# Two attention and expert layers on one core: the expert stage in two parts, its tiles in the order of steps of the attention

## The reference: what is computed

```python
# attention of layer 0; layer 1 has biases and the mask for rope
q = (x @ Wq).reshape(B, Nq, H, hd).transpose(0, 2, 1, 3)
kv = (context @ Wkv).reshape(B, Nkv, 2, H, hd).transpose(2, 0, 3, 1, 4)
q, k, v = _apply_rope(q), _apply_rope(kv[0]), kv[1]
attn = jax.nn.softmax(jnp.einsum('bhqd,bhkd->bhqk', q, k) * scale, axis=-1)
out = jnp.einsum('bhqk,bhkd->bhqd', attn, v).transpose(0, 2, 1, 3).reshape(B, Nq, C) @ Wo + bo

# experts of layer 0
probs = jax.nn.softmax(tokens @ Wr + br, axis=-1)
expert = jnp.argmax(probs, axis=-1)
h = jax.nn.relu(jnp.einsum('td,edh->teh', tokens, W1) + b1[None])
y = jnp.einsum('teh,ehd->ted', h, W2) + b2[None]   # the row of `expert`, times its probability

# experts of layer 1
topk_vals, topk_idx = jax.lax.top_k(gate_logits, 2)
probs = jax.nn.softmax(topk_vals, axis=-1)
g = jax.nn.silu(jnp.einsum('btc,hc->bth', x, w_gate_proj[e]))
u = jnp.einsum('btc,hc->bth', x, w_up_proj[e])
out = out + jnp.einsum('bth,ch->btc', g * u, w_down_proj[e]) * w_e[..., None]

# the whole
x = x + tanh(g_xattn[0]) * L0_xattn(layernorm(x), ctx)        # rotary q and k, softmax over 77 keys
x = x + tanh(g_ffn[0])   * L0_ffn(layernorm(x))               # best expert: relu(t @ W1 + b1) @ W2 + b2, times its probability
x = x + tanh(g_xattn[1]) * L1_xattn(layernorm(x), ctx, mask)  # biases, a mask
x = x + tanh(g_ffn[1])   * L1_ffn(layernorm(x))               # two best experts: (silu(g) * u) @ Wd, weighted
```

## Time and profile before

| | us |
|---|---|
| median of three runs | 472.65 (469.25 to 473.23) |
| the profiled execution | 466.07 |
| its span in the trace | 464.2 |
| PE busy | 314.7 (68%) |
| DVE busy | 264.1 (57%) |
| POOL busy | 152.2 (33%) |
| ACT busy | 136.3 (29%) |
| data moved | 52.93 MB, mean 114 GB/s |

### The profile page before, as it was taken

How to read it: one execution, slowest core, us unless ns; L and a number is a source line. 1 busy time by engine, 2 the same in 40 slices (tenths; PEclk the granted TensorE clock), 3 DMA queues, 4 the chain that set the end, 5 groups by cost and what they waited for, 6 DMA issues and landing times.

```text
span 464.2 us, 7008 instructions
## 1 busy us (share of the span) xinstructions
PE 314.7 (68%) x1932; PEld 228.1 (49%) x1932; DVE 264.1 (57%) x916; ACT 136.3 (29%) x302; POOL 152.2 (33%) x172
## 2 busy tenths in 40 slices
PE   2468999989754095751467999999530298888920
PEld 2236555545353094640256566654320297777820
DVE  2768668773675244353367667765545066665634
ACT  2412354535313033220103454354200033333300
POOL 3211212051423134561102102165766134555550
PEclk9767799999985579795567999999855599999985
DMA  7434032100000867823231313000103677988708
GB/s 268 126 74 118 12 80 52 43 11 19 17 8 29 224 215 215 243 73 90 62 85 36 71 27 85 14 24 23 42 29 100 213 244 236 299 249 289 235 12 269
DMA packets 39997, 52.93 MB, mean 114 GB/s; under 512 B 7177, under 2 KB 24334, under 8 KB 39968
## 3 DMA queue, kind: packets, MB, share of 16 engines
q1 hardware_dynamic: 33648, 45.03, 33.7%
q0 software_dynamic: 3584, 6.36, 3.9%
q10 hardware_dynamic: 2736, 1.20, 0.9%
HBM read 35.58 MB, written 9.64 MB: 97 GB/s over the span
## 4 chain that ended last, share of the span: by engine, by line
PE 21%; DVE 8%; issue 7%; DMA 6%; SPq 4%; POOL 4%; ACT 1%; POOLq 0%; DVEq 0%; ACTq 0%
POOL routed L445 3%; PE ps_s L750 2%; PE ps_a L730 2%; DMA xt<-routed 2%; PE ps_a L731 2%; PE ps_s L821 2%; SPq L342 2%; PE ps_s L751 2%; PE ps_t L705 2%; PE ps_n L765 2%; PE ps_a L838 1%; PE ps_d L765 1%; PE ps_t L821 1%; DMA probs<-expert_out 1%; DMA routed<-pay,slot 1%
## 5 line engine op out<-in xcount | busy, mean ns | idle before, releaser
L463 POOL DMA_INDIRECT expert_out<-yo,rows_at x64 | 63.0, 984 | 81.5 <-DVE yo L1179 63.6
L529 ACT ACTIVATE probs<-ps_s 103x512 f32<-103x512 f32 (+1 forms) x96 | 56.3, 597 | 56.8 <-PE ps_s L751 53.3
L445 POOL DMA_INDIRECT routed<-pay,slot x48 | 48.4, 1009 | 58.3 <-DVE slot L1132 47.8
L1025 DVE TENSOR_REDUCE negm<-ps_a 128x4 f32<-128x308 f32 x128 | 55.1, 470 | 19.5 <-PE ps_a L731 18.0
L750 PE MATMUL ps_s<-qs,ks 128*103 128x512 f32 (+1 forms) x96 | 46.2, 481 | 2.0 <-ACT augT L522 1.2
L731 PE MATMUL ps_a<-ks,qs 128*128 128x308 f32 x128 | 43.1, 374 | 5.9 <-DVE negm L1025 5.6
L421 POOL TENSOR_SCALAR ve<-mv 128x4 f32<-128x4 f32 x16 | 4.0, 251 | 116.0 <-DVE mv L975 116.0
L751 PE MATMUL ps_s<-augT,aug 128*103 128x512 f32 (+1 forms) x96 | 39.6, 412 | 0.0
L838 PE MATMUL ps_a<-cst,xt 128*128 128x128 f32 x32 | 11.1, 355 | 39.8 <-DMA xt<-routed 38.2
L731 PEld LDWEIGHTS ps_a<-ks,qs 128*128 128x128 f32 x128 | 28.9, 227 | 15.4 <-DVE negm L1025 6.6
L821 PE MATMUL ps_s<-xT,probs 128*128 128x128 f32 x208 | 32.5, 299 | 2.9 <-DVE xT L1190 1.7
(11 more groups left out here) (168 smaller groups left out, 659.3 us busy)
## 6 DMA issues: line engine op xcount, KB each, us to landing
probs<-f_in SPq DMA_DIRECT2D x40, 384.0 KB
qs<-qhl SPq DMA_DIRECT2D x128, 64.0 KB, 2.0
probs<-f_in SPq DMA_DIRECT2D x24, 321.0 KB
xt<-routed SPq DMA_DIRECT2D x32, 65.0 KB
probs<-routed SPq DMA_DIRECT2D x32, 65.0 KB
yin<-expert_out SPq DMA_DIRECT2D x8, 256.0 KB, 4.4
routed<-pad ACTq DMA_DIRECT2D x18, 65.0 KB
x<-x_in SPq DMA_DIRECT2D x4, 256.0 KB, 7.6
```

The costliest lines, as they stand in the source:

```text
L445: pool.indirect_dma_start(out=routed[l], out_offset=bass.IndirectOffsetOnAxis(ap=slot[c][:, t:t + 1], axis=0), in_=pay[c][:, t, :], in_off ...
L463: pool.indirect_dma_start(out=expert_out[l], out_offset=bass.IndirectOffsetOnAxis(ap=rows_at[i % SHORT][:, :], axis=0), in_=yo[i % SHORT][ ...
L529: nc.scalar.activation(probs[n % 2][0:KSIZE[j], s, :], ps_s[(NS * n + s) % SCORE_BANKS][0:KSIZE[j], :], ACT.Exp, scale=SCALE).then_inc(exp ...
L1025: nc.vector.tensor_reduce(negm[:, i, g * HPG:(g + 1) * HPG], a[:, 0:GK].rearrange("p (h k) -> p h k", h=HPG), AX.X, ALU.max, negate=True). ...
```

## The change

There is one list of steps for the whole program, and layer 1's step 0 is step 102 of it (`SECOND`). Each layer's expert stage is cut into two parts of two batches, with its own `routed` table, counts, plan and pad rows. Parts 0 and 1 have 15 tiles each, parts 2 and 3 have 23 each. Tile t of part p is at step `TILE_AT[p]` + t, with TILE_AT 51, 74, 153 and 178, and each engine does its piece at the end of its step. The loops are gone: all 76 tiles are written out.

Part 0 stands in the steps of the last batch's tail of layer 0, part 1 in those of the front of layer 1, part 2 in the last batch's tail of layer 1, and part 3 alone at the end. The key and value work of layer 1 moves some steps back, and its keys go through the ring of banks.

`probs` is one buffer: batch n's exponentials overwrite a third of it once batch n - 1 has weighed that third. The second buffer's place goes to `fw`, now a tile array of its own, as are `hid` (2), `yb` (2), `xt` (10, was 8). The turned rows and the down product share a bank (`turn_bank`), up goes to the two score banks. Weights are asked for 5 steps ahead of a tile, rows 4 steps ahead. POOL reads the row numbers in `xt` itself. Pad rows move from ACT's queue to SP's. In layer 1 ACT scales the output. The q buffers are doubled. Results of batches 0 and 1 of layer 1 are loaded, added and stored within part 3.

```diff
+PARTS = 4
+PART_NB = 2
+TILES = [(PART_TOKENS * CHOICES[p // 2] + E * (P - 1)) // P for p in range(PARTS)]
+SECOND = 102
+TILE_AT = [51, 74, SECOND + 51, SECOND + 76]
+WEIGHTS_AHEAD, ROWS_AHEAD = 5, 4
+RETURN_AT = TILE_AT[2] + TILES[2] + LAG_OUT + 4
+END = TILE_AT[3] + TILES[3] + LAG_OUT
-KEYS_SPREAD_AT = [-18, LAST + 24]
-VALUES_AT = [[-2, -1, 0], [LAST + 17, LAST + 20, LAST + 21]]
-BLOCKS_AT = [-17, LAST + 27]
+KEYS_SPREAD_AT = [-18, LAST + 34]
+VALUES_AT = [[-2, -1, 0], [LAST + 35, LAST + 37, LAST + 39]]
+BLOCKS_AT = [-17, LAST + 37]
...
+            def load_weights(p, t):
+                l, j = p // 2, FIRST[p] + t
+                if t == 0:
+                    sp.wait_ge(meta_ok, p + 1)
...
+                if j >= SLOTS:
+                    sp.wait_ge(f_y, j - SLOTS + 1)
...
+            def load_rows(p, t):
+                j = FIRST[p] + t
+                if t == 0:
+                    for n in range(PART_NB * p, PART_NB * (p + 1)):
+                        sp.wait_ge(scattered[n], 16 * TPB * CHOICES[p // 2])
+                    sp.wait_ge(padded[p], 16 * (E + 1))
...
+                if j >= ROWS:
+                    sp.wait_ge(f_put[(j - ROWS) % SHORT], puts_through(j - ROWS + 1, (j - ROWS) % SHORT))
...
+            for k in STEPS:
+                for p in plans(k):
+                    pad_rows(p)
+                for n in due("results", k):
+                    if n >= NB:
+                        load_results(n - NB)
...
+                    for t in range(TILES[p]):
+                        if k == TILE_AT[p] + max(-1, t - ROWS_AHEAD):
+                            load_rows(p, t)
+                for n in due("low", k):
+                    spread_q(n)
...
-                if n >= 2 and s == 0:
-                    act.wait_ge(pv_ok, KT * (n - 1))
+                if n and g == 0:
+                    act.wait_ge(pv_ok, KT * (n - 1) + j + 1)
...
+            def turn_and_down(p, t):
...
+                if t < TILES[p]:
...
+                    pe.wait_ge(r_ld[j % ROWS], 16 * (j // ROWS + 1))
+                    last = nc.tensor.transpose(bank[:, 0:P], rows_of(j)[:, 0:D], ident)
+                if t >= LAG_DOWN:
+                    pe.wait_ge(f_hid, d + 1)
...
+                for p, t in tile_steps(k):
+                    if t >= LAG_OUT:
+                        put_tile(p, t - LAG_OUT)
```

807 lines of the change are left out of this document (396 added, 411 removed).

## The result

The changed kernel is slower: 493.64 us median (489.19 to 498.0, 4 runs) beside 470.95 for the kernel before (464.37 to 473.23, 4 runs), ratio 1.054 with a 95% interval of 1.036 to 1.073. Run again beside the experiments, on a chip where the kernel before takes 463.09 us, the ratio was 1.060 (1.052 to 1.068). The forecast was 408 us. The executions of one kernel spread by some 3%, the longer ones mostly at a lower granted clock, so the ratios compare the quicker ones alone, but for e2's, while the medians are over all.

A forecast was written before the change was run, and what follows sets the result against it. Tails were taken to wait on latency and tiles on loads, laid end to end. Gains of 39.6 and 21.4 us took the span from 464.2 to 403.2; 405.1 as execution, 410.8 scaled, so 408 us was predicted, range 388 to 432.

The forecast's parts named there:

- What bounds the kernel: Whole kernel: tails wait on latency, tiles on loads, different kinds of work laid end to end; attention offers nothing to win.
- More tiles: Expert stages: 76 tiles for 64; the 12 extra cost 22.5 us if nothing hides them.
- Part 0 beside the tail: Layer 0's last tail: chain plus 15 tiles take 38 us to part 1's first tile, bounds 34 and 61.
- Part 1 beside the front: Layer 1's front: 30.6 us of tile steps, 4 of SP stall, 8 of maxima and split; gain 39.6 us.
- At nothing: Probs ring, q buffers and other small parts cost nothing; plans 0 and 2 1 us each, against 2 us for PE's clock.
- Not longer by more than 3 us: Attention: the forecast would be wrong if it got longer by more than 3 us.
- Part 2 beside the tail: Layer 1's last tail: POOL's scatters and puts come last, at 381 us; bounds 368 and 413.
- Part 3 and the end: End of layer 1: 26 steps at 1.8 us, 47 us, to 428, then 15 us; end at 442.8.
- (c): Tails and tiles: nothing overlaps, extra tiles paid whole, less 14 us for loop turns; about 485 us, chance 0.04.
- (a): Tails: hops stall the tiles on in-order engines, half of each hidden stretch paid, 19 us more; about 427, chance 0.18.
- (b): Tile stream quicker: straight code saves loop-turn stalls, 1.7 us a tile in layer 1, tails at chain length; about 390, chance 0.18.
- (d): Layer 1's front: SP's queue is the bound, scores come behind both spreads, 18 us later; about 426, chance 0.08.

The follow-up runs named there:

- e2: Changed kernel with parts 0 and 2 begun 15 steps later, behind their layer's last tail and plan; ratio to the kernel before 1.066.
- e10: Changed kernel with 12, 12, 20 and 20 tiles in place of 15, 15, 23 and 23; 468.62 us, ratio to the kernel before 1.013.
- e5: Changed kernel with VectorE's four additions of layer 0's results each three steps later; ratio to the kernel before 1.036.
- e6: Changed kernel with each tile's rows loaded five steps ahead in place of four; ratio to the kernel before 1.042.
- e8: Changed kernel with e1, e5, e6 and e7 together, and parts 2 and 3 fifteen steps later; ratio to the kernel before 0.990.
- e14: Kernel of e11 with the plan of part 0 two steps later; 446.06 us, ratio to the kernel before 0.957.
- e1: Changed kernel with the results of batch 3 loaded ahead of the third spread's 16 copies on SP's queue; ratio to the kernel before 1.026.
- e11: Layer 0 as in e8, layer 1 as one part of 39 tiles behind its last plan; 452.08 us, ratio to the kernel before 0.974.
- e9: The changed kernel unaltered, measured again beside other experiments; 490.28 us, ratio to the kernel before 1.060.
- e4: The kernel before with its expert loops written out, nothing else changed; 463.36 beside 462.03 us, ratio 0.999.
- e12: Kernel of e11 with matmuls nobody reads put into TensorE's idle stretches; 451.72 us, ratio to the kernel before 0.975.
- e15: Kernel of e14 with the filler matmuls of e12; ratio to the kernel before 0.961.
- e7: Changed kernel with six output buffers of the tiles in place of four; ratio to the kernel before 1.062.

## Why the prediction was wrong, step by step

*What bounds the kernel.* The reading of the earlier trace rows was right as far as it went: PE was busy 15.7 of 40 us. The step from there to "work of different kinds can lie side by side" was the mistake. A low share of busy time says that an engine waits; it does not say that its program can take something else meanwhile.

*More tiles, 22.5 us.* Right: 21.7 us (e10). The words "if nothing hides them" were the case that came.

*Part 0 beside the tail, 38 us from the first hop to part 1.* The term failed at "a quarter to a third of a us for each" hop. From 127.8 to 187.05 are 59 us, nearly the upper bound of 61 that I had computed and dismissed. 5 of the 21 us too many come ahead of the first hop (the plan of part 0, and TensorE at 1.2 GHz behind it); the rest is tiles: the plan comes 17.7 us later than with none beside it (e2, 33.8 for 51.5), 1.2 us for each of 15 tiles where I booked some 0.3. In e2 their turns alone span 28.5 us; 7.5 us are hidden at part 1's first tile.

*Part 1 beside the front, 43 us.* The mechanism on SP was foreseen, its size was not: the last row load did stand behind the first spread. Priced at 4 us, it was a gap of 9.4 between two turns. What I did not follow is the second link: tile late, so ACT's next copy late, so second spread late, so the results of batch 2 late, so DVE's maxima late. e5 is worth 13 us and e6 4.5; with both (e8, e14) the stretch takes 47 and 44 us for 62.4. That is near the 43, but attention then takes 5 to 8 us more than the 76.0 of e1, because the wait for batch 2's results has only moved; no run has both. The issue of 0.63 us a copy is what cost here, as the row said, against the Trainium skill's rule (DMA: Bandwidth & Descriptors, Issuing engines are not separate DMA queues) that I had weighed beside it.

*At nothing.* The probs ring and the two query buffers were right: with e1 attention takes 76.0 us. The plans at 1 us each were wrong; in layer 0 and 1 the tail begins 5.1 and 4.0 us late. A little over 2 us in each is PE's longer wait, the rest TensorE at its lower level behind it, which the sum did not have; a plan moved by two steps keeps 4.1 of the 5.1 (e14), and without a plan there (e11, layer 1) the 4.9 us are those of before. The 2 us that I booked for the clock were for another place, the start of layer 1. "Not longer by more than 3 us" failed by 12, for the load behind the third spread, which I had not placed at all.

*Part 2 beside the tail, 56 us to part 3.* It took 89.0, near the upper bound of 88 (413 at a last exponential of 325). "The rows and weights are fetched during attention" failed first: the second batch's row copies end behind the last exponential, so the first turn stood 15.6 us behind it, not 3 to 6, and the tail's ranks behind that turn. POOL's sum of scatters and puts was not what came last. The plan itself was late, 63.0 for 30.5, with PE busy 37 of 47 us at a clock of 0.76. Of the 32.5 us, 2.8 are there without tiles too (e2, 33.3), 4.0 are the wait for the first tile's rows, and 25.7 the 18 tiles, 1.4 each where I had booked 13 us for all of them (381 for 368). Another 13.5 us lie between plan and part 3 (26.0 for 12.5): POOL starts the last scatter 76.8 us behind the last exponential (35.7 before), and SP then has part 3's weights to load, into buffers that are not free, ahead of its rows.

*Part 3 and the end, 62 us.* Right: 60.7 (63.3 in e9), though at 1.95 us a tile for the 1.8 booked, and so by luck in part.

*The rivals.* (c), given 0.04, is the case that came, 485 for a median of 493.64, and its deciding point was right: fewer than 23 us of tiles are hidden. Not all of its terms were: there was no gain of 14 us from loop turns (e4), and in their place stood the queue on SP. (a) held for the mechanism, at the full price and not half of it. (b) loses its main reason by e4, and with it what I drew for this case from the Trainium skill's rule on taken branches (Runtime: NRT & Kernel Launch, Instruction fetch mechanics): no run here shows a cost of the loop. (d) had the right place: the results of batch 2 behind the second spread.

*Left open.* Why a tile costs 1.4 us of the tail in layer 1 and 1.2 in layer 0 when each engine is busy half of the time or less but for PE; how much of it is TensorE's clock of 0.76; and three waits of ACT in and behind layer 1's tail (3.2, 3.5 and 5.3 us), which end at an event that the profile does not name. Of the 8.0 us by which e14's attention (84.0) is longer than e1's, the wait that moved is 6.4; the rest was not followed.

## What to carry to other kernels

Two chains in the same in-order programs add up unless the trace shows otherwise: book the sum, and hold a gain from overlap for proven only where each step of the one has a slot free of the other (here, from plan to plan, 1.65 us a tile at every step, 1.1 where the first eight stood at every second one, 1.9 alone). Look first at what the first piece waits for, since everything behind it in the same program waits along: one tile turned before its rows were there cost layer 1's tail 4 us. When a load moves into another order of issues, walk the queue to its end and then follow each late item to the engine that waits for it and to what is queued behind that wait; one 0.5 us load behind 16 issues cost 12 us. And a split in parts that each round up costs the rounded work in full: split only the layer in which there is something to lay beside it. Here that is layer 0, whose second part lies beside the next layer's front; the kernels with only layer 0 split (e11, e12, e14, e15) are the fastest. None was run with both layers whole and the rest of the change kept, so what layer 0's split alone is worth is not shown.

## What the runs showed of the hardware

A single wait that disappears can be worth next to nothing: e7 took away 3.29 us and the work behind it came 0.6 us sooner. Sixteen copies issued by one engine hold its queue 10.0 to 10.3 us. TensorE's granted clock rose from 0.836 to 0.869 by filler matmuls without any gain in time (e11, e12). Elsewhere the clock did cost time: the same 31 matmuls took PE 7.3 us at a granted clock of 0.50 (1.2 GHz), behind waits of 3.91 us (changed) and 2.95 (e14), and 4.2 us at 1.00 (2.4 GHz), behind one of 1.81 (before), and the chain of the tail was 3.0 us longer for it. Writing out loops of 8 tiles changed nothing, 0.999 (0.993 to 1.005).
